# Scan of a selective state space layer: who finishes a tile, how many buffers, and when the sums are taken

## The reference, cut to what matters

```
x = silu(causal_conv(xn @ in_w.T))                 # 800 x 1024
delta = softplus(x @ wd1.T @ wd2.T + wd2_b)
B, C = x @ wB.T, x @ wC.T                          # 16 states
h = exp(delta * A) * h + (delta * x) * B           # step by step, for each of 16 states
y = sum over the 16 states of C * h, + W_D * x
out = (y * silu(xn @ skip_w.T)) @ out_w.T
```

## Time and profile before

| | us |
|---|---|
| median of three runs | 2684.29 |
| the profiled execution | 2690.38 |
| its span | 2688.6 |
| PE busy in the span | 2418.4 (90%) |
| DVE busy | 1368.0 (51%) |
| ACT busy | 911.2 (34%) |
| POOL busy | 622.9 (23%) |

### The profile page before, as it was taken

One profiled execution on the slowest core, in us unless ns is written; L12 is line 12 of the kernel. 1 busy time (PEld: TensorE's weight loads), 2 busy tenths in 40 slices (PEclk: granted clock), 3 DMA queues, 4 the chain that ended last, 5 costly groups with the idle time before them and its releaser, 6 DMA issues. The chain is left out here.

```text
span 2688.6 us, 31765 instructions
## 1 busy us (share of the span) xinstructions
PE 2418.4 (90%) x11965; PEld 1243.1 (46%) x11965; DVE 1368.0 (51%) x1957; ACT 911.2 (34%) x1868; POOL 622.9 (23%) x523
## 2 busy tenths in 40 slices
PE   7899999889999999888599799886998679999996
PEld 4444444344555555536345454353674333333332
DVE  5699999423788886731445512286444521111114
ACT  3666665114533334401122110086333212222221
POOL 0577878200000000001201100000000024444342
PEclk9999999889999999998789899998999789999998
DMA  3732222444545445336600100112000162560634
GB/s 108 235 106 84 82 94 76 109 185 155 181 144 170 161 126 150 102 109 221 215 12 0 43 0 4 38 59 94 1 1 4 66 244 84 214 277 27 241 116 144
DMA packets 96587, 301.31 MB, mean 112 GB/s; under 512 B 27018, under 2 KB 57446, under 8 KB 81724
## 3 DMA queue, kind: packets, MB, share of 16 engines
q1 hardware_dynamic: 62784, 171.06, 19.1%
q0 software_dynamic: 33664, 128.35, 13.2%
HBM read 446.13 MB, written 47.22 MB: 183 GB/s over the span
## 5 line engine op out<-in xcount | busy, mean ns | idle before, releaser
L758 POOL TENSOR_TENSOR x_rows<-ms_state,mb_C_everywhere 128x800 f32<-128x800 f32 x128 | 239.8, 1885 | 159.7 <-DVE ms_state L726 115.3
L1019 PE MATMUL psum<-at_Wv,at_context 128*128 128x512 f32 (+1 forms) x576 | 266.1, 601 | 0.0
L781 PE MATMUL psum<-mb_context,mb_key_w 128*128 128x361 f32 x768 | 253.2, 479 | 7.1 <-PEq L835 6.2
L726 DVE TENSOR_TENSOR_SCAN ms_state<-ms_decay,psum 128x800 f32<-128x800 f32 x128 | 233.0, 1820 | 12.4 <-ACT ms_decay L675 6.9
L3035 PE MATMUL psum<-tf_W,tf_x_T 128*64 128x512 f32 x1024 | 228.9, 600 | 0.8 <-DVE tf_x_T L3098 0.8
L3089 ACT ACTIVATE tf_hidden<-psum,tf_b 128x64 f32<-128x64 f32 x512 | 108.3, 362 | 357.2 <-PE psum L3046 357.2
L3057 PE MATMUL psum<-tf_W,tf_hidden 128*64 128x512 f32 x1024 | 226.1, 594 | 0.0
L781 PEld LDWEIGHTS psum<-mb_context,mb_key_w 128*128 128x128 f32 x768 | 141.6, 191 | 121.8 <-issue 34.0
L1120 ACT ACTIVATE at_prob<-psum,at_neg_max 100x722 f32<-100x722 f32 x128 | 110.4, 863 | 145.8 <-DVE at_neg_max L1182 145.6
L2970 POOL DMA_INDIRECT tf_W<-in_L_W,tt_weight_row x120 | 119.4, 995 | 164.0 <-PE psum L3035 118.7
L1182 DVE TENSOR_REDUCE at_neg_max<-psum 100x1 f32<-100x722 f32 x128 | 115.7, 904 | 78.3 <-PE psum L1040 77.9
(11 more groups left out here) (483 smaller groups left out, 3680.8 us busy)
## 6 DMA issues: line engine op xcount, KB each, us to landing
at_piece<-in_L_W_f POOLq DMA_DIRECT2D x24, 1024.0 KB, 6.4
keys_dram<-x_rows SPq DMA_DIRECT2D x128, 180.5 KB, 1.9
at_k_cols<-keys_dram SPq DMA_DIRECT2D x64, 361.0 KB, 3.2
sf_W<-in_L_W SPq DMA_DIRECT2D x16, 1024.0 KB, 7.4
tf_W<-in_L_W SPq DMA_DIRECT2D x8, 2048.0 KB, 20.0
mb_context<-in_ctxT SPq DMA_DIRECT2D x16, 541.5 KB, 4.7
at_context<-in_ctxT SPq DMA_DIRECT2D x8, 1083.0 KB, 5.4
ternary_dram<-at_piece_made POOLq DMA_DIRECT2D x14, 512.0 KB
```

What stands on the lines that cost most here:

```text
L726: nc.vector.tensor_tensor_scan(state[:, n % RH, :], decay[:, g % RA, :, :].rearrange("p b l -> p (b l)"), drive, 0.0, ALU.mult, ALU.add).t ...
L758: nc.gpsimd.tensor_tensor(seen[:, n % RV, :], state[:, n % RH, :], cC[:, n, :], ALU.mult).then_inc(weighed, 1)
L781: last = nc.tensor.matmul(side("key", u, t == KE - 1)[:, 0:SH], lhsT=wk[:, k, e * P:(e + 1) * P], rhs=keys[:, h, k, :], start=(k == 0), st ...
L1019: last = nc.tensor.matmul(bank[0:rows_of(t), :], lhsT=ctxT[:, b % 2, k, t * P:t * P + rows_of(t)], rhs=wv[:, k, h * BANK:(h + 1) * BANK], ...
```

## The change

1. Finishing a tile is split. ScalarE copies the sums from PSUM into the conv columns at state 5 of the next tile (four copies of 64 x 400, counted in `copied`), and GpSimd multiplies them by the gate in SBUF at state 2 of its own order. The last tile is finished by VectorE as before.
2. Three buffers of weighed states instead of two.
3. Five joins a tile, JOIN = [1, 3, 5, 7, 9], instead of four: 11 sums and the skip term.
4. The sums trail: block m sums states 2m-3 and 2m-2.
5. TensorE waits for `copied` instead of `finished` before it opens the bank y again.
6. The weights of delta are no longer all in SBUF: two tiles' worth are, and SP loads one tile's 32 KB two tiles ahead. SP's loop over tiles is written out.

```diff
...
             delta = sb2("delta", [P, 2, T])
-            proj, wd2 = sb2("proj", [PROJ, T]), sb2("wd2", [PROJ, E_IN])
+            proj, wd2 = sb2("proj", [PROJ, T]), sb2("wd2", [PROJ, 2, P])
             keys, ctx_loaded = sb2("context", [P, 2, KC, SH]), [c.sem(f"mb_context_loaded_{h}") for h in range(2)]
...
             sp.dma_start(projw[:, :, :], dram["L0_proj_w"]).then_inc(proj_loaded, 16)
-            sp.dma_start(wd2[0:DR, :], dram["L0_wd2"]).then_inc(proj_loaded, 16)
+            sp.dma_start(wd2[0:DR, :, :].rearrange("p z e -> p (z e)"), dram["L0_wd2"][:, 0:2 * P]).then_inc(proj_loaded, 16)
             sp.dma_start(wk[:, :, :], dram["L0_Wkv"][:, :, 0:INNER]).then_inc(wk_loaded, 16)
...
                 prod.wait_free(pe, len(tiles) + h)
-                nc.tensor.matmul(prod.bank(h)[:, 0:HALF], lhsT=wd2[:, 0:P],
+                nc.tensor.matmul(prod.bank(h)[:, 0:HALF], lhsT=wd2[:, 0, :],
                                  rhs=proj[:, half(h)], start=True, stop=True).then_inc(prod.filled, 1)
...
             own = Chain(dve, chain_s)
-            nc.vector.memset(wd2[DR:PROJ, :], 0.0).then_inc(wd2_padded, 1)
+            nc.vector.memset(wd2[DR:PROJ, :, :], 0.0).then_inc(wd2_padded, 1)
             turned.grant(dve)
...
     nc, dram = c.nc, c.dram
-    RA, RH, RV, RS = 4, 4, 2, 2
+    RA, RH, RV, RS = 4, 4, 3, 2
     with ExitStack() as ctx:
...
         skipw = free[:, 0:D].rearrange("p (k e) -> p k e", k=KD)
-        gate, seen = part(0, 1), part(1, RV).rearrange("p (r t) -> p r t", r=RV)
+        gate, seen = part(0, 1), [part(1, 1), part(2, 1), sb("seen", [P, T])[:, :]]
         made = free[:, D + 3 * T:D + 3 * T + 2 * SH].rearrange("p (r s) -> p r s", r=2)
...
         summed = sem("summed")
-        finished = sem("finished")
-        gated = sem("gated")
+        copied, finished = sem("sums_copied"), sem("finished")
+        gated, wd2_loaded = sem("gated"), sem("wd2_loaded")
         half = lambda h: slice(h * HALF, (h + 1) * HALF)
...
-        FINISH, SCALE, SUM_X, OPEN = 1, 6, 5, 11
+        COPY_AT, FINISH, SCALE, SUM_X, OPEN = 5, 2, 6, 5, 11
         GATE_AT, DELTA_AT, LAG = [2, 3], [0, 1], 2
...
         ends_block = lambda n: n % 2 == 1
-        JOIN = [3, 5, 7, 9]
+        JOIN = [1, 3, 5, 7, 9]
+        TRAIL = 3
         input_made = lambda t: t * (1 + N_ST) + 1
...
         def sums_through(t, n):
-            return t * SUMS + sum(a + 1 not in JOIN for a in range(n + 1)) if n >= 0 else sums_through(t - 1, n + N_ST)
+            return t * SUMS + sum(a + 1 not in JOIN for a in range(n + 1))
+
+        slot = lambda t, n: seen[(t * N_ST + n) % RV]
...
+            def load_wd2(t):
+                sp.dma_start(wd2[0:DR, t % 2, :], dram["L0_wd2"][:, t * P:(t + 1) * P]).then_inc(wd2_loaded, 16)
+
             def store(t, first=False, last=False):
+                if t + 2 < KE:
+                    load_wd2(t + 2)
                 for u in range(N_ST):
...
             load_skip(0)
-            store(0, first=True)
-            with sp.Fori(0, KE - 2) as t:
-                store(t + 1)
-            store(KE - 1, last=True)
+            for t in range(KE):
+                store(t, t == 0, t == KE - 1)
             for r in range(2):
...
                 ins.then_inc(curved, 1)
+
+            def copy_sums(t):
+
+                act.wait_ge(summed, (t + 1) * SUMS)
+                for r, h in quads:
+                    at = placed(r, h)
+                    ins = nc.scalar.copy(xc[at, t, half(h)], y[r][at, :])
+                ins.then_inc(copied, 1)
...
                         take_gate(t, GATE_AT.index(taken // 2), last)
+                    if n == COPY_AT and not first:
+                        copy_sums(t - 1)
                     if n in CURVE_AT and not last:
...
         def _(dve):
-            def finish(i, j):
-
-                dve.wait_ge(summed, (i * 2 + j) * SUMS)
-                dve.wait_ge(gated, i * 2 + j)
+            def finish_last():
+
+                dve.wait_ge(summed, KE * SUMS)
+                dve.wait_ge(gated, KE)
                 for r, h in quads:
                     at = placed(r, h)
-                    last = nc.vector.tensor_tensor(xc[at, bass.ds(i * 2 + j - 1, 1), half(h)].rearrange("p a t -> p (a t)"),
-                                                   y[r][at, :], gate[at, half(h)], ALU.mult)
-                last.then_inc(finished, 1)
+                    nc.vector.tensor_tensor(xc[at, KE - 1, half(h)], y[r][at, :], gate[at, half(h)], ALU.mult).then_inc(finished, 1)
...
                                                      drive, 0.0, ALU.mult, ALU.add).then_inc(scanned, 1)
-                        if n == FINISH and not (first and j == 0):
-                            finish(i, j)
                 own.close()
...
                 turn(i + 1, False)
-            finish(TURNS, 0)
+            finish_last()
...
                         pool.wait_ge(chain_s, input_made(t + 1))
-                    if (n - 1) % N_ST in JOIN and t + n:
-                        pool.wait_ge(joined, joins(t, n - 1) + 1 if n else t * len(JOIN))
-                    elif t or n >= RV:
-                        pool.wait_ge(summed, sums_through(t, n - RV))
-                    nc.gpsimd.tensor_tensor(seen[:, n % RV, :], state[:, n % RH, :], cC[:, n, :], ALU.mult).then_inc(weighed, 1)
+                    if g + i * per >= RV:
+                        held, was = divmod(i * per + g - RV, N_ST)
+                        if was + 1 in JOIN:
+                            pool.wait_ge(joined, joins(held, was + 1) + 1)
+                        else:
+                            pool.wait_ge(summed, sums_through(held, was))
+                    nc.gpsimd.tensor_tensor(slot(t, n), state[:, n % RH, :], cC[:, n, :], ALU.mult).then_inc(weighed, 1)
                     if n in JOIN:
                         pool.wait_ge(weighed, i * per + g + 1 + RH)
-                        nc.gpsimd.tensor_tensor(seen[:, n % RV, :], seen[:, n % RV, :], seen[:, 1 - n % RV, :], ALU.add).then_inc(joined, 1)
+                        nc.gpsimd.tensor_tensor(slot(t, n), slot(t, n), slot(t, n - 1), ALU.add).then_inc(joined, 1)
+                    if n == FINISH and t:
+                        pool.wait_ge(copied, t)
+                        pool.wait_ge(gated, t)
+                        nc.gpsimd.tensor_tensor(xc[:, t - 1, :], xc[:, t - 1, :], gate, ALU.mult).then_inc(finished, 1)
                     if last and j == 1:
...
                 pe.wait_ge(side_taken, at_side(t, False, "delta", h) + 1)
-                nc.tensor.matmul(side("delta", h)[:, 0:HALF], lhsT=wd2[:, (t + 1) * P:(t + 2) * P], rhs=proj[:, half(h)],
+                if h == 0 and t:
+                    pe.wait_ge(wd2_loaded, 16 * t)
+                nc.tensor.matmul(side("delta", h)[:, 0:HALF], lhsT=wd2[:, (t + 1) % 2, :], rhs=proj[:, half(h)],
                                  start=True, stop=True).then_inc(side_filled, 1)
...
             def add_state(t, n):
-                if n == 0:
-                    pe.wait_ge(finished, t + 1)
+                if n == 0 and t:
+                    pe.wait_ge(copied, t)
                 if n + 1 in JOIN:
                     return
+                opens = sums_through(t, n) == t * SUMS + 1
                 if n in JOIN:
...
                     pe.wait_ge(weighed, t * N_ST + n + 1 + RH)
-                add(lambda p, cols: seen[p, n % RV, cols], n == 0, n == N_ST - 1).then_inc(summed, 1)
+                add(lambda p, cols: slot(t, n)[p, cols], opens, n == N_ST - 1).then_inc(summed, 1)
...
                     add(lambda p, cols: xc[p, t, cols], False, False)
-                for g in range(t * N_ST + 2 * m - 2, t * N_ST + 2 * m):
+                for g in range(t * N_ST + 2 * m - TRAIL, t * N_ST + 2 * m - TRAIL + 2):
                     if g >= 0:
...
                     block_of(t, m)
-            for n in range(N_ST - 2, N_ST):
+            for n in range(N_ST - TRAIL, N_ST):
                 add_state(KE - 1, n)
```

## The result

The changed kernel takes 2695.25 us, the median of 9 runs, beside 2685.59 us for the kernel before (9 runs): ratio 1.003, 95% interval 1.0017 to 1.0043. That is some 8 us slower by the ratio, 9.7 between the medians. On another chip, in 12 runs beside 29, the ratio was 1.0015 (1.0003 to 1.0026). I had forecast 3.7 us faster.

The account below looks back on a forecast made before the run. A four-engine loop bounds the kernel; after the change, TensorE and ScalarE at 49.9 us a tile against 50.1. Six loops -1.5, finishing -2.1, slots -0.5, a meeting +0.35 give -3.7: 2684.29 to 2680.6 us, own range 2675 to 2686.

Parts of the forecast that it names:

- (3): TensorE, block 1: new wait for ScalarE's four copies stalls it 1.96 us a tile, bounds 1.8 and 3.5.
- (1): VectorE: finishing leaves it, saving 2.12 us a tile in seven tiles, so it needs 48.0 us.
- (2): TensorE: trailing sums and five joins remove join waits (2.1 us a tile) and 0.84 of sums, leaving 47.2 us.
- (4): TensorE before key 12: ScalarE's chain to the copy of key 10 now shows, +0.8 us a tile.
- (5): GpSimd: a fifth join and the gating product raise it from 39.4 to 43.1 us a tile, at no cost.
- (6): Third buffer, loads of delta's weights and SP's unrolled loop: no effect on the time.
- (7): Tile 0, held by transfers: taken as 0, with ends of -1.5 and +0.5 us.
- (8): The end: six loops -1.5, finishing of tile 6 -2.1, third slot -0.5, a product meeting a weighing +0.35; together -3.7 us.
- Rival A: Copies are hidden and the tile falls to VectorE's 48.0 us: -15.3 us, 2669; chance 0.14.
- Rival C: Block 1: TensorE's new wait costs 3.5 us a tile, more than join waits gave back: +6 us, 2690; chance 0.10.
- Rival B: The stall is there but ScalarE's chain before key 12 gives way; loop 49.1 us: -8 us, 2676; chance 0.15.
- Rival D: Finishing's gain lost to GpSimd's order at state 2 and long first products on VectorE, up to 13 us; chance 0.05.

Follow-up runs that it names:

- the four profiles: Four profiled executions of the changed kernel, no edits: scans (first product to end of last finish) of 410.8, 410.5, 413.1 and 410.9 us.
- three products: Changed kernel with three extra key-shaped products on TensorE, overwritten by key 4, ahead of its wait for the copies in block 1: 2690.54 us, ratio 0.9992.
- by one: Changed kernel with one extra key-shaped product on TensorE ahead of its wait for the copies in block 1: 2689.19 us, ratio 0.9988.
- key 10 ahead of decay 12: On top of the late wait, ScalarE copies key 10 before decay 12 instead of behind it: 2676.28 us, ratio 0.9938 to the kernel before.
- the late wait: Changed kernel with TensorE's wait for the copies moved from block 1 to the first sum that needs the bank, in block 2: 2679.66 us, ratio 0.9948.
- the runs in which VectorE finishes: As the late wait, but VectorE finishes each tile as before, without ScalarE's copies or GpSimd's gating product: 2687.8 us, ratio 0.999.

## Why the prediction was wrong

**The step that failed is (3), the price of the stall.** I priced it by its own length, 1.96 us, and let what follows run as before. The stall was 2.09 us, but it had a second term behind it: in 18 of 28 tiles of the four profiles the granted clock fell and keys 4 and 5 took up to 1.7 us more (5.4 to 5.6 for 3.9). In the first profile that is 4 x 1.7 = 6.8 us: forecast 408.2 - 3.7 = 404.5, and 404.5 + 6.8 = 411.3, measured 410.8. With the clock held by three products or by one the scan was 404.0 and 403.8. I could have asked: the earlier trace rows gives the granted clock, and the longest wait of TensorE in the rows of those tiles was 1.61 us, so no row showed what 2 us would do. That should have widened the bounds of the term.

The Trainium skill, TensorE: Matmul & The Clock Gate, section "What's actually happening", says that the clock is gated by how busy the engine has lately been. The runs agree: the same wait with three products ahead of it left the granted clock at 1.00 over tiles 2 to 6.

- The bound, a loop of TensorE and ScalarE, was right: 49.92 us where the clock holds, 49.9 forecast.
- (1), (2): right. TensorE waits for no join in tiles 2 to 6, where the waits were 10.0 us. Finishing off VectorE is worth 7.8 us of scan once TensorE does not stand for it, the rest 4.9 to 5.3.
- (4): right, 0.73 us before key 12 (0.8), and removable, as key 10 ahead of decay 12 shows.
- (5), (6): right for the tiles, no cost of GpSimd's 43.1 us a tile.
- (7): tile 0 took 50.3 to 51.1 us in the four profiles, 51.7 and 51.2 before: inside the ends that I gave, a little below the 0.
- (8): in the run with three products the whole of (1) to (8) came to a scan 3.8 to 4.2 us shorter, for 3.7. Its 0.35 for a meeting in the last tile did not come: the first product there took 0.97.
- Rival A asked for the copies to be hidden. With the late wait they are, and the gain is 14 us (A: 15.3). Rival C had the place and nearly the price (3.5 a tile; it was 3.8 in slow tiles, 2.1 in the others), but by dear copies, which they were not. I gave it 0.10. Rival B is out: TensorE does wait before key 12. Rival D is out: the first products of tiles 2 to 7 took 0.97 us. Only that of tile 1 was longer, 1.24 in the first profile, as before (1.32 at 140.25). A wait up to the weighing's end would have made that one 1.43, so "it stood until GpSimd was done" is off by 0.1 us.

Left open is the rest of the time. The medians moved by 9.7 us on one chip and 5.5 on another (8 and 4 by the ratios); the four scans are 2.7 to 5.3 us above the mean of the two of before (407.8). The mean granted clock of a whole execution, which unprofiled runs have too, was 0.9467 in the 12 runs of the changed kernel and 0.9495 in the 29 beside them. By my estimate the difference, 0.0028 of 2695 us, is 7.5 us, or 4.4 clock falls of 1.7 us each, and the four profiles have 4.5 slow tiles on the mean. It is a rough estimate: the runs in which VectorE finishes had 0.9483 with no slow tile in their profile, some two falls lower. So the unprofiled runs seem to have about as many slow tiles as the profiled ones, which leaves up to 2 us on one chip and 4 to 6 on the other unexplained. Why an equal stall is followed by a fall in one tile and not in the next is open too.

## What to carry to other kernels

Of a wait on the engine that bounds the loop, ask what it has queued between the last thing it gave and the wait: copies of 1.9 us cost nothing beside two keys, and right behind the last sum all their length and more. A new stall of TensorE can have two prices, its length and the clock after it. Here the second turned a small gain into a loss. A wait belongs at the first instruction that needs it, not at the state where the tile begins.

## What the runs showed of the hardware that I had not expected

In front of keys 4 and 5, standing 1.28 us never cost TensorE its clock (0 of 6 tiles). Standing 2.09 us did in 17 of 24 tiles, 1.99 in 1 of 4, and 3.99 or 3.90 in 7 of 7. In the same execution equal stalls went both ways. The keys that followed lost up to 1.7 us after 2.09 us and up to 2.8 after 3.99.
